# Summing the wide items of the later chunks on GpSimd, in halving additions behind a tile's gathers

## The chip, the cores and the metric

The program runs on one core of one Trainium2 chip. The metric is the device time of one execution, in microseconds (us). The engines are TensorE (PE in the rows, PEld its weight loads), VectorE (DVE), ScalarE (ACT), GpSimd (POOL) and SyncE (SP, which here only issues DMAs).

## The reference

2048 samples with 40 embedding fields of width 64 each. Every pair of fields goes through a 64x64 matrix of its own, and the results go with 16 dense numbers into a small tower:

```python
e = jnp.stack([tbl_0[ids[:, 0]], ..., tbl_39[ids[:, 39]]], axis=1)      # 2048 x 40 x 64
p = inputs[:, rowidx]                                                  # 780 pairs (i < j)
q = inputs[:, colidx]
out = jnp.einsum('bie,fie,bif->bi', p, param, q)                       # param 64 x 780 x 64
h = jnp.concatenate([z, dense_ctx], axis=1)
h = jnp.maximum(h @ W_top1 + b_top1, 0.0)
h = jnp.maximum(h @ W_top2 + b_top2, 0.0)
y = h @ W_top3
```

All of it is in float32.

## The kernel before

The batch is cut into 4 chunks (0 to 3) of 512 samples. Two fields make a tile, so a chunk has 20 tiles; tiles are numbered through the chunks (tile 33 is number 13 of chunk 1). All engines have their instructions written out in program order, and walk through one list of 800 items, 200 in a chunk: 136 "units" and 64 "wides" (v = 0 to 63), which `order(c)` spreads among the units, one wide in about every three items.

**An item** is two matrix products of TensorE into two banks of a ring of 7 PSUM banks (lines 793 and 798), and two multiplications of VectorE that read the banks (lines 668 and 671 for a unit, 685 for a wide). So TensorE can be 7 banks, three and a half items, ahead of VectorE. The products of a unit are summed by TensorE with a matrix of ones (line 816). The products of a wide lie with the samples on the partitions: 128 partitions x 16 columns x 64 elements in `wide_prod`, and the 64 elements have to be summed to one, 16 sums per partition, into `z_b`. Line 606 does that on ScalarE, in 16 activations with an accumulator, four items behind the product. Where `reduced_by_vector` says so, VectorE does it in one TENSOR_REDUCE (line 696) one item behind the product. In chunks 1 to 3 that is every eighth wide: v = 7, 15, 23, 31, 39, 47, 55, 63.

**The slots of wide_prod.** There are 4 (`WIDE_SLOTS`), taken in turn. Before VectorE multiplies wide v + 4 it waits in `wait_reduced` until wide v is summed. VectorE works in order, so whatever stands behind that product waits too.

**The gathers.** GpSimd fetches the rows of a tile with 8 indirect DMAs (line 537), 4 for each of the tile's fields, and waits after each 4 until they have landed. Tiles 4 to 19 of a chunk share three slots of `rows`. Before it gathers into a slot again, GpSimd waits until SyncE's transposing DMA (line 466, semaphore `words_turned`) has read the tile that was in it, three tiles earlier. SyncE issues that transpose from `turn_rows`, no earlier than its place among the weight loads, and those follow TensorE's progress; then four DMAs make planes (line 476), and ScalarE turns them into `e_t` (line 563), which the products read. GpSimd does nothing else after the first microseconds.

Of the kernel before, what the change touches and what calls it, by code (L numbers as in the profile page):

```python
# [8 lines left out]
ALU = mybir.AluOpType  # L9
# [3 lines left out]
P = 128  # L13
E = 64
# [6 lines left out]
CHUNKS = BATCH // NB  # L21
# [6 lines left out]
FIXED = 4  # L28
# [5 lines left out]
WIDES = [(m, t) for m in range(FIXED, TILES) for t in range(BT)]  # L34
NW = len(WIDES)
WIDE_PAIRS = 4 * FIXED
# [6 lines left out]
G_SLOTS = 3  # L43
# [3 lines left out]
WIDE_SLOTS = 4  # L47
# [10 lines left out]
HALVES = WIDE_PAIRS * (TILES - FIXED) // P  # L58
# [24 lines left out]
FIRST_TURNED = 9  # L83
TURN_AHEAD = 10
# [15 lines left out]
def order(c):  # L100

    units = [("unit", u) for u in range(NU)]
    wides = [("wide", v) for v in range(NW)]
    head = sum(m < FIXED for m, _ in UNITS)
    if c > 0:

        items = units[:head]
        spread = NU - head - BEHIND_LAST
        for v in range(NW - 1):
            items += [wides[v]] + units[head + spread * v // (NW - 1):head + spread * (v + 1) // (NW - 1)]  # L110
        return items + [wides[-1]] + units[head + spread:]


    hot = [item for item in units if UNITS[item[1]][0] in ONE_HOT]
    items = hot + units[:head]
    for m in range(FIXED, TILES):
        row = [item for item in units if UNITS[item[1]][0] == m and item not in hot]
        for t in range(BT):
            items += [wides[(m - FIXED) * BT + t]] + row[len(row) * t // BT:len(row) * (t + 1) // BT]
    return items  # L120


ORDERS = [order(c) for c in range(CHUNKS)]
# [3 lines left out]
PLACE = {item: n for n, item in enumerate(ITEMS)}  # L127
# [53 lines left out]
def through(n):  # L181

    return 2 * (n + 1)
# [36 lines left out]
def prep_at(tile):  # L220

    c, m = divmod(tile, TILES)
    if c == 0:

        first = FIRST_OF[0, 5 if m == 4 else max(m, 1)]
        return first if m <= ONE_HOT[-1] else first - m
    return c * NI + TILE_AT[m]
# [24 lines left out]
def reduced_by_vector(c, v):  # L252

    m, t = WIDES[v]
    return c == 0 and (t == 3 and m < 12 or t == 1 and m < 8) or c > 0 and v % 8 == 7


def fixed_slot(c):
# [19 lines left out]
def by_dma(tile):  # L278
    return tile >= FIRST_TURNED
# [5 lines left out]
DMA_TILES = [tile for tile in TILE_ORDER if by_dma(tile)]  # L285
DMA_NUMBER = {tile: n for n, tile in enumerate(DMA_TILES)}
GATHERED = [tile for tile in range(ALL_TILES) if tile not in ONE_HOT]
TILES_AT = {}
for _t in TILE_ORDER:
    TILES_AT.setdefault(prep_at(_t), []).append(_t)  # L290
STEPS_AT = {(_c + 1) * NI + STEP_AT[_s]: (_c, _s) for _c in range(CHUNKS - 1) for _s in range(STEPS)}
# [15 lines left out]
def bank_plan():  # L307
# [3 lines left out]
    for n in range(ALL_ITEMS):  # L311
        takers += [("tile", t) for t in TILES_AT.get(n, ()) if not by_dma(t)]
        if n in STEPS_AT:
# [41 lines left out]
def bilinear_tower(nc, tables, idx, hot_ids, dense_t, weights, w1z, b1c, w2p, b2c, w3c, out):  # L355
    with ExitStack() as ctx:
# [6 lines left out]
        def sem(name):  # L363
            return ctx.enter_context(nc.semaphore(name))
# [9 lines left out]
        wide_prod = sb("wide_prod", [P, WIDE_SLOTS, 2, NB])  # L374
        z_b = sb("z_b", [P, HALVES, BT, P])
# [39 lines left out]
        t_free = sem("t_free")  # L415
        summed = sem("summed")
        reduced_s = sem("reduced_s")
        reduced_v = sem("reduced_v")
        turned = sem("turned")
        z_copied = sem("z_copied")  # L420
        step_ps = sem("step_ps")
# [5 lines left out]
        def wait_reduced(engine, wides):  # L427

            by_vector = sum(reduced_by_vector(*divmod(v, NW)) for v in range(wides))
            if by_vector:  # L430
                engine.wait_ge(reduced_v, by_vector)
            if wides > by_vector:
                engine.wait_ge(reduced_s, wides - by_vector)

        def fields(tiles, slots, t):

# [74 lines left out]
        @block.gpsimd  # L511
        def _(pool):
            nc.gpsimd.memset(ident[:, :], 0.0).then_inc(consts, 1)
            pool.wait_ge(consts, 1)
            nc.gpsimd.affine_select(out=ident[:, :], in_=ident[:, :], compare_op=ALU.not_equal, fill=1.0,
                                    base=0, pattern=[[-1, P]], channel_multiplier=1).then_inc(consts, 1)
            nc.gpsimd.iota(first_row[:, :], [[1, 1]], base=0, channel_multiplier=HOT_J).then_inc(rows_known, 1)
            pool.wait_ge(idx_in, 16)
            for tile in GATHERED:
                c, m = divmod(tile, TILES)  # L520
                slot, use = slot_of(tile)
                if c > 0 and m == 0:
                    pool.wait_ge(idx_in, 16 * (c + 1))
                if m < FIXED and use > 1:

                    pool.wait_ge(t_free, through(PLACE[c - 2, "wide", NW - 1]))
                elif use > 1:

                    last = max(t for t in GATHERED if t < tile and slot_of(t)[0] == slot)
                    if by_dma(last):  # L530
                        pool.wait_ge(words_turned, 16 * (DMA_NUMBER[last] + 1))
                    else:
                        pool.wait_ge(transposed, PE_NUMBER[last] + 1)
                for f in range(2):
                    for t in range(BT):
                        col = (m * 2 + f) * BT + t
                        nc.gpsimd.indirect_dma_start(  # L537
                            out=fields([tile], slice(slot, slot + 1), t)[:, 0, f, :], out_offset=None, in_=tables[m * 2 + f],
                            in_offset=bass.IndirectOffsetOnAxis(ap=idx_now[:, c % 2, col:col + 1], axis=0),
                        ).then_inc(gathered[slot], 16)  # L540
                    if c > 0 or m > 0 or f > 0:

                        pool.wait_ge(gathered[slot], 16 * BT * (f + 1 + 2 * (use - 1)))

        @block.scalar
        def _(act):
# [78 lines left out]
            for n in range(ALL_ITEMS + max(GROUP_LAG) + 1):  # L625
                for tile in TILES_AT.get(n, ()):
                    prepare(tile)
                if n == NI:
                    act.wait_ge(mlp_in, (4 + ZT) * 16)
                if n in STEPS_AT:  # L630
                    finish_step(*STEPS_AT[n])
                if n in TURNS_AT and n < ALL_ITEMS:
                    copy_half(TURNS_AT[n])
                for c, t in Z_ORDER:
                    if t < ZS and group_at(c * GROUPS + Z_FIRST[t + 1] - 1) == n:
                        copy_z(c, t)
                done = n - REDUCE_LAG
                if 0 <= done < ALL_ITEMS and ITEMS[done][1] == "wide":
                    c, _, v = ITEMS[done]
                    if not reduced_by_vector(c, v):  # L640
                        reduce(c, v)
            for half in range(HALVES_ALL):
                if turn_at(half) >= ALL_ITEMS:
# [1 line left out]
            c = CHUNKS - 1  # L645
# [85 lines left out]
        def _(pe):  # L731
# [120 lines left out]
            for n, (c, kind, i) in enumerate(ITEMS):  # L852
                for tile in TILES_AT.get(n, ()):
                    if tile in ONE_HOT:
# [122 lines left out]
```

## Time and profile before

| | us |
|---|---|
| median of the timed runs (3 runs) | 1218.11 |
| lowest and highest | 1217.02, 1220.1 |
| span of the profiled execution | 1255.3 |
| PE busy | 1224.6 (98%) |
| DVE busy | 1053.7 (84%) |
| ACT busy | 972.3 (77%) |
| POOL busy | 573.2 (46%) |

The profiled execution's span, from its first to its last instruction, is 37.2 us longer than the median of the timed runs; no time around the span is given. Times in the rows are us from the start of the span. TensorE's busy time counts overlapped and waiting products and its ends are modelled, so 98% does not mean that it never waits.

### The profile page before, as it was taken

Reading aid. Unit: us, or ns where it says so; the run is one execution under the profiler, and the core shown is the slowest. Engines: PE = TensorE matmul, PEld = TensorE weight load, DVE = VectorE, ACT = ScalarE, POOL = GpSimd, SP = SyncE. Lnnn points to the kernel's source line nnn. Section 1 sums busy time; section 2 is a strip of 40 time slices with the busy share of each in tenths; the row PEclk is TensorE's granted clock in tenths of the full one; section 3 lists DMA queues with packets and bytes.
Section 4 is the critical chain, followed back from the end, with each engine's and each line's share of the span. In section 5 each row is a group of like instructions: output and inputs, shape, how many; then the busy total and the mean of one; then the engine's idle time right before and its main releaser. Section 6 shows DMA issues by size and latency. Waiting matters only on the chain.

```text
span 1255.3 us, 22898 instructions
## 1 busy us (share of the span) xinstructions
PE 1224.6 (98%) x5808; PEld 476.8 (38%) x5808; DVE 1053.7 (84%) x1720; ACT 972.3 (77%) x7177; POOL 573.2 (46%) x607
## 2 busy tenths in 40 slices
PE   6989999999999999999999999999999999999999
PEld 3323433333333333333333433334333334333333
DVE  6858899988888797889998888788999878899980
ACT  0019999975868887898968988799968988899951
POOL 5655554455455555555245555555245555400000
PEclk9988899999999999999999999999999999999999
DMA  7033344433544333333454433333353434122100
GB/s 207 18 113 104 79 119 117 110 104 92 140 100 120 102 104 87 88 81 97 106 134 106 113 84 94 87 80 96 95 155 90 114 97 111 49 63 83 44 1 1
DMA packets 132098, 118.87 MB, mean 95 GB/s; under 512 B 91351, under 2 KB 110039, under 8 KB 131965
## 3 DMA queue, kind: packets, MB, share of 16 engines
q1 hardware_dynamic: 111188, 94.94, 27.3%
q0 software_dynamic: 19200, 19.70, 7.6%
q10 hardware_dynamic: 1576, 2.76, 0.8%
q8 instruction: 46, 0.75, 0.3%
q14 instruction: 88, 0.71, 0.2%
HBM read 80.09 MB, written 0.01 MB: 64 GB/s over the span
## 4 chain that ended last, share of the span: by engine, by line
PE 88%; ACT 7%; issue 2%; DVE 2%; DMA 1%; SPq 0%; ACTq 0%; DVEq 0%
PE ring L793 40%; PE z_ps L816 18%; PE ring L798 17%; PE ring L822 8%; ACT wide_prod L606 6%; PE ring L756 2%; PE ring L826 2%; DVE prod L671 1%; DMA z_t<-tbl 1%; DVE wide_prod L685 0%; ACT e_t L567 0%; PE ring L774 0%; PE ring L829 0%; ACT h L620 0%; PE ring L767 0%
## 5 line engine op out<-in xcount | busy, mean ns | idle before, releaser
L606 ACT ACTIVATE wide_prod<-wide_prod 128x64 f32<-128x64 f32 x3520 | 841.8, 242 | 55.1 <-DVE wide_prod L685 34.8
L537 POOL DMA_INDIRECT rows<-tbl,idx_now x600 | 572.4, 954 | 514.9 <-DMA rows<-tbl,idx_now 310.0
L671 DVE TENSOR_TENSOR prod<-ring,e_t 128x512 f32<-128x512 f32 x1008 | 630.6, 683 | 114.3 <-PE ring L793 97.0
L606 ACT ACTIVATION_READ_ACCUMULATOR wide_prod<-wide_prod 128x1 f32 x3520 | 662.6, 188 | 17.8 <-issue 17.1
L793 PE MATMUL ring<-e_t,w 64*128 64x512 f32 x2176 | 584.3, 613 | 13.6 <-issue 4.8
L685 DVE TENSOR_TENSOR wide_prod<-ring,rows 128x512 f32<-128x512 f32 x512 | 327.8, 682 | 32.1 <-PE ring L798 12.8
L793 PEld LDWEIGHTS ring<-e_t,w 64*128 64x128 f32 x2176 | 229.0, 187 | 326.0 <-issue 210.0
L798 PE MATMUL ring<-w,e_t 64*128 64x512 f32 x1024 | 305.8, 616 | 4.2 <-DVE wide_prod L685 1.8
L816 PE MATMUL z_ps<-prod,strip 128*32 128x512 f32 x2096 | 253.9, 598 | 0.0
L798 PEld LDWEIGHTS ring<-w,e_t 64*128 64x128 f32 x1024 | 116.2, 189 | 150.5 <-issue 85.9
L816 PEld LDWEIGHTS z_ps<-prod,strip 128*32 128x32 f32 x2096 | 55.0, 109 | 179.7 <-issue 117.0
L822 PE MATMUL ring<-z_t,w 128*128 128x512 f32 x224 | 99.8, 598 | 0.0
L563 ACT ACTIVATE e_t<-planes 128x1024 uint16<-128x1024 uint16 x71 | 82.3, 1163 | 12.1 <-DMA planes<-words 12.1
L822 PEld LDWEIGHTS ring<-z_t,w 128*128 128x128 f32 x224 | 41.4, 190 | 56.8 <-issue 47.6
L668 DVE TENSOR_TENSOR prod<-ring,e_t 64x512 f32<-64x512 f32 x80 | 54.8, 685 | 5.9 <-PE ring L793 2.9
L567 ACT ACTIVATE e_t<-ring 128x512 f32<-128x512 f32 x9 | 5.3, 596 | 69.3 <-PE ring L756 38.8
L579 ACT ACTIVATE z_t<-z_ps 128x512 f32<-128x512 f32 x20 | 11.8, 592 | 52.2 <-PE z_ps L816 42.6
L756 PE MATMUL ring<-wide_prod,z_t 125*64 125x512 f32 x160 | 37.6, 618 | 10.7 <-DMA z_t<-tbl 10.3
L696 DVE TENSOR_REDUCE z_b<-wide_prod 128x16 f32<-128x1024 f32 x36 | 43.5, 1209 | 0.0
L615 ACT ACTIVATE h<-ring,b 128x512 f32<-128x512 f32 x16 | 11.0, 686 | 38.8 <-PE ring L822 37.1
L713 DVE TENSOR_SCALAR wide_prod<-w,first_row_f 125x512 f32<-125x512 int32 x56 | 24.5, 492 | 11.4 <-DMA z_t<-tbl 7.9
L826 PE MATMUL ring<-h,w 128*128 128x512 f32 x64 | 29.2, 602 | 0.0
(24 smaller groups left out, 76.4 us busy)
## 6 DMA issues: line engine op xcount, KB each, us to landing
w<-weights SPq DMA_DIRECT2D x64, 768.0 KB
planes<-words SPq DMA_DIRECT2D x284, 64.0 KB
rows<-tbl,idx_now POOLq DMA_INDIRECT x600
z_t<-tbl SPq DMA_DIRECT2D x10, 224.0 KB
w<-weights SPq DMA_DIRECT2D x4, 512.0 KB
w<-hot_ids ACTq DMA_DIRECT2D x7, 256.0 KB
w<-w1z SPq DMA_DIRECT2D x7, 256.0 KB
words<-rows SPq DMA_TRANSPOSE x71
```

What stands on the lines that cost most here:

```text
L537: nc.gpsimd.indirect_dma_start(out=fields([tile], slice(slot, slot + 1), t)[:, 0, f, :], out_offset=None, in_=tables[m * 2 + f], in_offset ...
L563: nc.scalar.activation(e_t[:, m, :].bitcast(U16).rearrange("p (b h) -> p b h", h=2), planes[:, plane_slot, :, :].rearrange("p h b -> p b h ...
L606: last = nc.scalar.activation(products, products, ACT.Copy, accum_out=z_b[:, h, t, col:col + 1])
L668: nc.vector.tensor_tensor(dst[half, 0, :], ring[half, bank, :], e_t[half, m - 1 + j, :], ALU.mult).then_inc(t_free, 1)
L671: nc.vector.tensor_tensor(dst[:, j, :], ring[:, bank, :], e_t[:, k, :], ALU.mult).then_inc(t_free, 1)
L685: nc.vector.tensor_tensor(dst[:, j, :, :, :], src[:, bank, :, :, :], fields(fixed, slice(fixed_slot(c), fixed_slot(c) + FIXED), t), ALU.mu ...
L756: last = nc.tensor.matmul(dst[E * h:E * h + E, :], hot_table[2 * i + h][:, E * j:E * j + E], hot[number % len(hot)], start=j == 0, stop=j ...
L793: nc.tensor.matmul(dst, w[field, slot, P * o:P * o + P], e_t[field, m - 1 if diagonal and b == 0 else m, :], start=True, stop=True).then_i ...
L798: nc.tensor.matmul(dst, e_t[field, m, P * t:P * t + P], w[field, slot, P * o:P * o + FIXED * P], start=True, stop=True).then_inc(t_ready, 1)
L816: last = nc.tensor.matmul(z_ps[32 * col:32 * col + 32, :], strip[:, 30 - 2 * r:62 - 2 * r], prod[:, (c * NU + UNIT_PLACE[c][u]) % PROD_SLO ...
L822: return nc.tensor.matmul(dst, w1[:, t * H1 + P * h:t * H1 + P * h + P], z_t[:, Z_NUMBER[c, t] % Z_SLOTS, :], start=start, stop=stop)
L826: return nc.tensor.matmul(dst, w2[:, k, P * h:P * h + P], h1[:, k, :], start=k == 0, stop=k == KH1 - 1)
```

## The change

The wides v % 8 == 7 of chunks 1 to 3, 24 in all, are no longer summed by VectorE but by GpSimd: six TENSOR_TENSOR additions, in place, each of which adds the upper half of the columns to the lower half (32, 16, 8, 4, 2 and 1 elements wide, 16 columns each); the last writes `z_b`. Between them GpSimd waits for its own preceding addition. The six stand in GpSimd's program behind the eighth gather of a tile that `pool_behind` picks, and ahead of the wait for its landing. `wait_reduced` waits for a third semaphore.

```diff
 def reduced_by_vector(c, v):
     m, t = WIDES[v]
-    return c == 0 and (t == 3 and m < 12 or t == 1 and m < 8) or c > 0 and v % 8 == 7
+    return c == 0 and (t == 3 and m < 12 or t == 1 and m < 8)
+
+def reduced_by_pool(c, v):
+    return c > 0 and v % 8 == 7
...
+POOLED = [(c, v) for c in range(CHUNKS) for kind, v in ORDERS[c] if kind == "wide" and reduced_by_pool(c, v)]
+
+def pool_behind(c, v):
+    n = PLACE[c, "wide", v]
+    behind = max(t for t in GATHERED if t - G_SLOTS < FIRST_TURNED or prep_at(t - G_SLOTS) - TURN_AHEAD <= n + 1)
+    return min(behind + (2 if NW // 2 < v < NW - 1 else 0), GATHERED[-1])
...
             by_vector = sum(reduced_by_vector(*divmod(v, NW)) for v in range(wides))
+            by_pool = sum(reduced_by_pool(*divmod(v, NW)) for v in range(wides))
             if by_vector:
                 engine.wait_ge(reduced_v, by_vector)
-            if wides > by_vector:
-                engine.wait_ge(reduced_s, wides - by_vector)
+            if by_pool:
+                engine.wait_ge(reduced_p, by_pool)
+            if wides > by_vector + by_pool:
+                engine.wait_ge(reduced_s, wides - by_vector - by_pool)
...
+            def fold(c, v):
+                m, t = WIDES[v]
+                h, first = divmod((m - FIXED) * WIDE_PAIRS, P)
+                products = wide_prod[:, (c * NW + v) % WIDE_SLOTS, :, :].rearrange("p j (i e) -> p (j i) e", e=E)
+                if c > 0:
+                    pool.wait_ge(turned, (c - 1) * HALVES + h + 1)
+                pool.wait_ge(t_free, through(PLACE[c, "wide", v]))
+                width = E // 2
+                while width > 1:
+                    nc.gpsimd.tensor_tensor(products[:, :, 0:width], products[:, :, 0:width],
+                                            products[:, :, width:2 * width], ALU.add).then_inc(folded, 1)
+                    folds[0] += 1
+                    pool.wait_ge(folded, folds[0])
+                    width //= 2
+                nc.gpsimd.tensor_tensor(z_b[:, h, t, first:first + WIDE_PAIRS], products[:, :, 0], products[:, :, 1],
+                                        ALU.add).then_inc(reduced_p, 1)
...
                         ).then_inc(gathered[slot], 16)
+                    if f == 1:
+                        for own in ADDED_AT.get(tile, ()):
+                            fold(*own)
                     if c > 0 or m > 0 or f > 0:
                         pool.wait_ge(gathered[slot], 16 * BT * (f + 1 + 2 * (use - 1)))
```

By `pool_behind` the additions for v = 7, 15, 23, 31, 39, 47, 55, 63 stand behind these tiles: in chunk 1 behind 33, 35, 38, 39, 42, 44, 46, 48; in chunk 2 behind 53, 55, 58, 59, 62, 64, 66, 68; in chunk 3 behind 73, 75, 78, and the last five all behind tile 79, the last one gathered.

On GpSimd, from the start of the program; all gathers merge into one row before:

```order
L513 MEMSET ident 128x128
L515 ISA
L515 AFFINE_SELECT ident<-ident 128x128
L517 IOTA first_row 128x1
L537 DMA rows<-tbl,idx_now 128x64 x600
L356 UNCONDITIONAL_BRANCH
```

The same place now, as far as the second group:

```order
L581 DMA rows<-tbl,idx_now 128x64 x232
L555 TENSOR_TENSOR wide_prod<-wide_prod 128x16x32
L555 TENSOR_TENSOR wide_prod<-wide_prod 128x16x16
L555 TENSOR_TENSOR wide_prod<-wide_prod 128x16x8
L555 TENSOR_TENSOR wide_prod<-wide_prod 128x16x4
L555 TENSOR_TENSOR wide_prod<-wide_prod 128x16x2
L560 TENSOR_TENSOR z_b<-wide_prod 128x16
L581 DMA rows<-tbl,idx_now 128x64 x16
```

Behind gather 232, the eighth of tile 33, six additions stand where the next gather stood; 16 gathers (tiles 34 and 35) then come before the next group.

On VectorE, around the sum of wide 7 of chunk 1, with the semaphores that each waits for, before (the first L685 row is the product of wide 7, the second that of wide 8):

```order
L685 TENSOR_TENSOR wide_prod<-ring,rows 128x512 [waits t_ready,reduced_s,reduced_v]
L685 TENSOR_TENSOR wide_prod<-ring,rows 128x512 [waits t_ready]
L671 TENSOR_TENSOR prod<-ring,e_t 128x512 [waits t_ready,summed]
L671 TENSOR_TENSOR prod<-ring,e_t 128x512 [waits t_ready]
L696 TENSOR_REDUCE z_b<-wide_prod 128x16 [waits t_free]
L671 TENSOR_TENSOR prod<-ring,e_t 128x512 [waits t_ready,summed]
L671 TENSOR_TENSOR prod<-ring,e_t 128x512 [waits t_ready]
L685 TENSOR_TENSOR wide_prod<-ring,rows 128x512 [waits t_ready,reduced_s,reduced_v]
```

On VectorE now, a little later: the product of wide 10, a unit, and the product of wide 11, which takes the slot of wide 7.

```order
L732 TENSOR_TENSOR wide_prod<-ring,rows 128x512 [waits t_ready,reduced_s,reduced_v]
L732 TENSOR_TENSOR wide_prod<-ring,rows 128x512 [waits t_ready]
L718 TENSOR_TENSOR prod<-ring,e_t 128x512 [waits t_ready,summed]
L718 TENSOR_TENSOR prod<-ring,e_t 128x512 [waits t_ready]
L732 TENSOR_TENSOR wide_prod<-ring,rows 128x512 [waits reduced_s,t_ready,reduced_p,reduced_v]
L732 TENSOR_TENSOR wide_prod<-ring,rows 128x512 [waits t_ready]
```

The TENSOR_REDUCE is gone, and the product of wide 11 is the first that waits for `reduced_p`, the last of GpSimd's six additions.

## Rows read from the trace of the kernel before

**Rows 1.** The page: engine busy times, and two groups (busy, mean ns; idle before, releaser).
```profile
PE 1224.6 (98%) x5808; PEld 476.8 (38%) x5808; DVE 1053.7 (84%) x1720; ACT 972.3 (77%) x7177; POOL 573.2 (46%) x607
...
L537 POOL DMA_INDIRECT rows<-tbl,idx_now x600 | 572.4, 954 | 514.9 <-DMA rows<-tbl,idx_now 310.0
...
L696 DVE TENSOR_REDUCE z_b<-wide_prod 128x16 f32<-128x1024 f32 x36 | 43.5, 1209 | 0.0
```

**Rows 2.** Timeline of VectorE in chunk 1 (start us, us, what): reduction of wide 7, later wides.
```profile
390.00 1.21 DVE L696 TENSOR_REDUCE z_b<-wide_prod 128x16 f32<-128x1024 f32 x1
...
392.32 1.28 DVE L685 TENSOR_TENSOR wide_prod<-ring,rows 128x512 f32<-128x512 f32 x2
...
399.24 1.28 DVE L685 TENSOR_TENSOR wide_prod<-ring,rows 128x512 f32<-128x512 f32 x2
...
403.07 1.28 DVE L685 TENSOR_TENSOR wide_prod<-ring,rows 128x512 f32<-128x512 f32 x2
...
406.88 1.28 DVE L685 TENSOR_TENSOR wide_prod<-ring,rows 128x512 f32<-128x512 f32 x2
```

**Rows 3.** Timeline of GpSimd: eighth gather of tile 33, first of tile 34.
```profile
423.31 0.95 POOL L537 DMA_INDIRECT rows<-tbl,idx_now  x1 [0.30 <-issue]
426.24 0.94 POOL L537 DMA_INDIRECT rows<-tbl,idx_now  x1 [1.98 <-DMA rows<-tbl,idx_now]
```

**Rows 4.** Timeline of GpSimd: eighth gathers of tiles 35 and 38.
```profile
449.44 0.95 POOL L537 DMA_INDIRECT rows<-tbl,idx_now  x1 [0.31 <-issue]
...
491.42 0.95 POOL L537 DMA_INDIRECT rows<-tbl,idx_now  x1 [0.30 <-issue]
```

**Rows 5.** Timeline of VectorE: products of wides 19 and 27 of chunk 1.
```profile
443.91 0.69 DVE L685 TENSOR_TENSOR wide_prod<-ring,rows 128x512 f32<-128x512 f32 x1
...
474.77 1.28 DVE L685 TENSOR_TENSOR wide_prod<-ring,rows 128x512 f32<-128x512 f32 x2
```

**Rows 6.** Timeline of GpSimd: first gathers of tiles 47, 49; eighth of 53, 58.
```profile
621.99 0.94 POOL L537 DMA_INDIRECT rows<-tbl,idx_now  x1 [22.03 <-DMA words<-rows]
...
652.65 0.94 POOL L537 DMA_INDIRECT rows<-tbl,idx_now  x1 [1.67 <-DMA rows<-tbl,idx_now]
...
716.36 0.94 POOL L537 DMA_INDIRECT rows<-tbl,idx_now  x1 [0.30 <-issue]
...
784.02 0.94 POOL L537 DMA_INDIRECT rows<-tbl,idx_now  x1 [0.30 <-issue]
```

**Rows 7.** Timeline of SyncE: the transpose of tile 44.
```profile
618.19 1.23 SPq L466 DMA_TRANSPOSE words<-rows  x1
```

**Rows 8.** Timeline of VectorE: products of wides 11 and 27 of chunk 2.
```profile
700.25 1.28 DVE L685 TENSOR_TENSOR wide_prod<-ring,rows 128x512 f32<-128x512 f32 x2
...
768.13 1.28 DVE L685 TENSOR_TENSOR wide_prod<-ring,rows 128x512 f32<-128x512 f32 x2
```

**Rows 9.** Timeline of GpSimd in chunk 3: eighth gathers of tiles 73 and 78.
```profile
1007.11 0.94 POOL L537 DMA_INDIRECT rows<-tbl,idx_now  x1 [0.30 <-issue]
...
1074.63 0.94 POOL L537 DMA_INDIRECT rows<-tbl,idx_now  x1 [0.30 <-issue]
```

**Rows 10.** Timeline of VectorE: products of wides 11 and 27 of chunk 3.
```profile
990.67 1.28 DVE L685 TENSOR_TENSOR wide_prod<-ring,rows 128x512 f32<-128x512 f32 x2
...
1058.37 1.28 DVE L685 TENSOR_TENSOR wide_prod<-ring,rows 128x512 f32<-128x512 f32 x2
```

**Rows 11.** GpSimd's other instructions, by group (busy, mean ns; idle before, releaser).
```profile
L515 POOL TENSOR_SCALAR_AFFINE_SELECT ident<-ident 128x128 f32<-128x128 f32 x1 | 0.3, 283 | 0.2 <-POOL ident L513 0.2
...
L517 POOL IOTA first_row<- 128x1 int32 x1 | 0.1, 119 | 0.0
```

**Rows 12.** Busy time by stretch: PE, PEld, DVE, ACT, POOL (count), clock, DMA, GB/s.
```profile
475.00:610.00 135.00, 134.42 (x636) 51.61 (x636) 114.39 (x185) 117.10 (x890) 69.81 (x75) 1.00 0.35 91
```

More of the change, by code:

```diff
@@ L287 @@
 GATHERED = [tile for tile in range(ALL_TILES) if tile not in ONE_HOT]
+POOLED = [(c, v) for c in range(CHUNKS) for kind, v in ORDERS[c] if kind == "wide" and reduced_by_pool(c, v)]
[3 more added lines that the diff above has]
+    return min(behind + (2 if NW // 2 < v < NW - 1 else 0), GATHERED[-1])
+ADDED_AT = {}
+for _c, _v in POOLED:
+    ADDED_AT.setdefault(pool_behind(_c, _v), []).append((_c, _v))
 TILES_AT = {}
@@ L418, in bilinear_tower @@
         reduced_v = sem("reduced_v")
+        reduced_p = sem("reduced_p")
+        folded = sem("folded")
         turned = sem("turned")
@@ L518, in _ @@
             pool.wait_ge(idx_in, 16)
+            folds = [0]
+            def fold(c, v):
[14 more added lines that the diff above has]
+                                        ALU.add).then_inc(reduced_p, 1)
             for tile in GATHERED:
@@ L639, in _ @@
                     c, _, v = ITEMS[done]
-                    if not reduced_by_vector(c, v):
+                    if not reduced_by_vector(c, v) and not reduced_by_pool(c, v):
                         reduce(c, v)
```

## The prediction, made before the changed kernel was run

> **What bounds the kernel now.** I read three views in this order. First the page's busy times [rows 1]: TensorE 98%, VectorE 84%, ScalarE 77%, GpSimd 46%. By these figures the change looks harmless: it takes 24 reductions of 1.209 us, 29.0 us, from VectorE and gives GpSimd, with half of its time free, some work. But the row of the gathers says what the free half is: 514.9 us of idle time, 310.0 of it waiting for gathers to land. GpSimd runs one dependent chain (four gathers, wait, four gathers, wait, next tile) and is late or early as a chain, however idle it looks.
>
> So the second view is the timeline of VectorE around one pooled wide [rows 2], and the third that of GpSimd at the tile behind whose gathers the additions now stand [rows 3]. The reader is to lay them side by side. In chunk 1 the reduction of wide 7 starts at 390.00. The L685 rows behind it are the products of wides 8, 9, 10 and 11, the last at 406.88. Wide 11 takes the slot of wide 7, so by then wide 7 has to be summed. The eighth gather of tile 33 ends at 423.31 + 0.95 = 424.26. That is 17.4 us after VectorE wants the slot, and the additions only begin there. VectorE works in order: behind the product of wide 11 stand all later items; TensorE fills its 7 banks and stops, and ScalarE runs out of products. GpSimd itself waits for nothing that this stalls (tiles 31 to 33 need only transposes that SyncE can issue at items well before wide 11), so the stall ends, but only when GpSimd's chain arrives.
>
> **What the six additions cost.** The trace has no TENSOR_TENSOR on GpSimd, so I bound it. They cover 16 x (32+16+8+4+2+1) = 1008 elements per partition. The nearest rows [rows 11] are a one-input pass over 128 elements, 283 ns, and one over a single element, 119 ns: 0.12 us fixed and (283 - 119)/127 = 1.3 ns per element. The same rows show 0.2 us for a handoff by semaphore between two GpSimd instructions; there are five between the additions and one to VectorE. Low end: at the one-input rate, 1.3 + 6 x 0.12 + 6 x 0.2 = 3.2 us. High end: each addition as long as a gather with its gap, 0.95 + 0.30, makes 7.5 us. I take two inputs at twice the one-input rate, 2.6 + 0.7 + 1.2 = 4.5 us, since that is the row nearest in kind. Call it F.
> The Trainium skill (page "GPSIMD Engine Reference", section "Performance versus the Vector engine") gives 4497 ns for an addition of 2048 float32 elements, 2.2 ns per element, and calls GpSimd the wrong engine for ordinary elementwise work. No row here shows it. Its rate would make F 4.1 us as an estimate, and the whole sum below 11 x 0.4 = 4.4 us smaller.
>
> What one group adds to GpSimd's own chain: before, the next tile's first gather came 1.98 us after the eighth [rows 3] (1.67 in [rows 6]; I use 2.0 with the longer ones among the others), spent on the landing, which now goes on beneath the additions. Then the next gather starts F + 0.3 after the eighth, so each group delays the chain by 4.5 + 0.3 - 2.0 = 2.8 us.
>
> **The sum, chunk by chunk,** as VectorE's delay against before.
> Chunk 1, wide 11: 424.26 + 4.5 - 406.88 = 21.9 us [rows 2, 3]. Wide 15 is summed behind tile 35: 450.39 + 2.8 + 4.5 = 457.7, and wide 19 would now start at 443.91 + 21.9 = 465.8 [rows 4, 5]: no new stall. Wide 23 stands behind tile 38: two groups ahead of it, 492.37 + 5.6 + 4.5 = 502.5, against 474.77 for wide 27 [rows 4, 5]. So VectorE is now late by 27.7 us; a second, smaller stall of about 6.
> In the rest of the chunk GpSimd is early, not late: at tile 47 it waits 22.03 us for the transpose of tile 44 [rows 6], issued at 618.19 [rows 7], which hangs on TensorE's progress. That wait survives: up to there GpSimd's chain is delayed by eight groups at most, or by waiting for products that come 27.7 us late, so it is about as late as VectorE, and the 22 us remain between them. From tile 47 on GpSimd again starts at a fixed distance behind TensorE: the delay of chunk 1 passes on whole, and chunk 2 repeats the pattern.
> Chunk 2, wide 11, with the group behind tile 48 ahead of it: 717.30 + 2.8 + 4.5 - 700.25 = 24.4 us; wide 27, with three groups ahead: 784.96 + 8.4 + 4.5 - 768.13 = 29.7 us [rows 6, 8].
> Chunk 3: 1008.05 + 2.8 + 4.5 - 990.67 = 24.7; 1075.57 + 8.4 + 4.5 - 1058.37 = 30.1 us [rows 9, 10]. Behind tile 79 nothing is gathered, so the last five groups only follow VectorE, each done 4.5 us behind its product with some 15 us to the slot's next use.
> Together 27.7 + 29.7 + 30.1 = 87.5 us.
>
> **What the removed reductions give back.** Those ahead of a stall give nothing, since GpSimd's arrival ends the stall. That leaves v = 31, 39, 47, 55 in each chunk and 63 in chunk 3: 13 x 1.2 = 15.6 us at most. In 475 to 610, VectorE is busy 114.4 of 135 us [rows 12]; there it also waits for TensorE at the tower's products, where a shorter VectorE changes nothing. I take two thirds, 10.4 us. Nothing is charged for GpSimd's additions against VectorE's speed; the bounds of F hold what little there may be.
>
> 87.5 - 10.4 = 77.1 us on the profiled 1255.3. The profiled execution is 3% slower than the timed ones; scaled by 1218.11/1255.3 = 0.970 this is 74.8 us, and 1218.1 + 74.8 = **1293 us**. The sum holds F eleven times (three in chunk 1, four in chunks 2 and 3): F = 3.2 gives 14 us less, F = 7.5 gives 33 more. With the share of the reductions between none and all (+10, -5) the case's own range is 1272 to 1325.
>
> **Rivals.**
> (a) The stalls are much shorter in a timed run than in the profiled one. The 37.2 us between the two need not be spread evenly. From the transpose of tile 44 at 618.19 to the eighth gather of tile 53 at 717.30 GpSimd's chain takes 99.1 us [rows 6, 7]; were it 10% faster when not profiled and VectorE not, each first stall would lose 10 us and the second nearly all: about 12 x 3 = 36 us less, 1257. For it: gathers are issued by GpSimd one by one and may suffer from being recorded. Against: more than 300 us of the chain are landings, which recording need not touch.
> (b) The additions are slow: F about 9, twice mine, because of narrow strided pieces (4, 2, 1 elements) or a change between gather and arithmetic code. Then 11 x 4.5 = 50 us more, plus a stall at wide 43 in each chunk, where VectorE's margin is a few us: about 1345. Against: 0.12 us fixed in [rows 11], and the first gather follows the IOTA without a reload that can be seen.
> The Trainium skill (same page, section "Architecture") says that the first call of freshly loaded code costs about 6 us with no visible instruction. No run here shows it; once, it would come through both stalls of chunk 1 as an estimated +6 us.
> (c) The other side: the stall does not come, since GpSimd reaches the groups in time, and the kernel gets faster. It takes a chain that is 22 us earlier at tile 33, 53 and 73; it decides where the eighth gather of tile 53 plus F falls before 700.25. Then VectorE's 29 us count at two thirds, 19.4, and the time is 1218 - 19 = 1199. Against: three chunks show the same lateness, 17.4, 17.1 and 17.4 us, in one trace, and waiting for the slot is in the program.
> (d) No change to be measured, with a stall that eats just the gain: no mechanism gives that but chance.
>
> **How the numbers follow.** Forecast 0.72, (a) 0.12, (b) 0.10, (c) 0.05, (d) 0.01. The predicted time is the forecast's, 1293. The range 1252 to 1325 holds the forecast's and (a)'s and leaves (b), (c) and (d) out. A measurement of this kernel tells about 0.3% (3.7 us) from no change. Faster: 0.05; within 0.3%: 0.01; slower: 0.94.
>
> **What would show it.** Right: VectorE idle for some 22 us at the product of wide 11 of chunks 1, 2 and 3 and some 6 us at wide 27, put down to GpSimd's last addition; six GpSimd additions that take 4.5 us from the first start to the last end and its handoff; 22 us of waiting at tile 47 still there; VectorE's busy time 29 us shorter. TensorE and ScalarE should show holes at the same places. Wrong: if VectorE's longest waits stay those for TensorE, or if the groups stand in the timeline before the product of wide 11 would come; if F is over 6 us, (b) is on; if the delay of chunk 1 shrinks again before tile 47, the passing on of delays was wrong.

## The result, and the profile after

| | us |
|---|---|
| before, median of 4 runs | 1218.16 |
| changed, median of 4 runs (1309.15 to 1319.41) | 1313.48 |
| ratio, 95% interval | 1.0756 (1.0695 to 1.0817) |
| forecast, range | 1293, 1252 to 1325 |

The change makes the kernel 95 us slower. The direction and the place were forecast; the size was 75 us in the forecast, and 20 us are to be explained. The profile of the changed kernel has a span of 1307.3 us. Its page, to be laid beside [rows 1]:

```profile
PE 1199.4 (92%) x5808; PEld 460.6 (35%) x5808; DVE 1025.7 (78%) x1696; ACT 962.2 (74%) x7177; POOL 649.5 (50%) x751
...
PE   6988999999982999999979699999969599999999
...
PEclk9988899999996999999989799999979799999999
...
L732 DVE TENSOR_TENSOR wide_prod<-ring,rows 128x512 f32<-128x512 f32 x512 | 327.4, 682 | 105.9 <-POOL z_b L560 55.5
```

The reader sees holes in TensorE's row of digits, dips of its granted clock at the same places, and a releaser that was not there before: VectorE's products of wides wait for GpSimd's last addition. VectorE's busy time is 28.0 us shorter, as its 24 missing reductions make it. Whom VectorE waited for in all (us, times, longest):

```profile
DVE prod L718 <- PE ring L840: 117.4, 76, 10.6
DVE wide_prod L732 <- POOL z_b L560: 55.5, 3, 24.9
DVE wide_prod L732 <- issue: 27.6, 8, 8.8
```

The first stall, where [rows 2] had the product of wide 11 at 406.88 with no wait and [rows 3] the eighth gather of tile 33. GpSimd's timeline:

```profile
414.21 0.94 POOL L581 DMA_INDIRECT rows<-tbl,idx_now  x1 [0.30 <-issue]
415.18 3.29 POOL L555 TENSOR_TENSOR wide_prod<-wide_prod 128x512 f32<-128x512 f32 x5
418.55 0.21 POOL L560 TENSOR_TENSOR z_b<-wide_prod 128x16 f32<-128x16 f32 x1
419.25 0.96 POOL L581 DMA_INDIRECT rows<-tbl,idx_now  x1 [0.49 <-issue]
```

VectorE's:

```profile
418.85 1.29 DVE L732 TENSOR_TENSOR wide_prod<-ring,rows 128x512 f32<-128x512 f32 x2 [24.95 <-POOL z_b L560]
```

The additions begin 0.03 us behind the eighth gather, end at 418.76, and VectorE goes on at 418.85: it was waiting for nothing else. The releaser column does not always say so: of the 27.6 us put down to "issue", 23.4 us are three waits at wide 27 (8.8, 7.7 and 6.8 us), and each ends 0.09 us behind a group of additions too. GpSimd's additions by shape (busy, mean ns of one; idle before):

```profile
L555 POOL TENSOR_TENSOR wide_prod<-wide_prod 128x512 f32<-128x512 f32 x24 | 30.5, 1273 | 130.1 <-DVE wide_prod L732 129.8
L555 POOL TENSOR_TENSOR wide_prod<-wide_prod 128x256 f32<-128x256 f32 x24 | 17.5, 728 | 1.9
...
L560 POOL TENSOR_TENSOR z_b<-wide_prod 128x16 f32<-128x16 f32 x24 | 5.1, 215 | 1.9
```

A group takes 3.6 us from first start to last end in each of its 24 places, where I had 4.5.

A wait that I had not forecast is TensorE's, at the turning of `z_b` (L821), where TensorE transposes the sums of the wides. It stands at item 405 for the second half of chunk 1, and at item 605 for that of chunk 2 (items are numbered 0 to 799 through the chunks). In chunk 1:

```profile
648.91 4.56 PE L840 MATMUL ring<-e_t,w 64*128 64x512 f32 x20
663.21 1.09 PE L821 MATMUL ring<-ident,z_b 128*128 128x128 f32 x4 [9.73 <-issue]
```

and on GpSimd, behind tile 48, the sum of wide 63:

```profile
659.51 3.30 POOL L555 TENSOR_TENSOR wide_prod<-wide_prod 128x512 f32<-128x512 f32 x5
662.89 0.21 POOL L560 TENSOR_TENSOR z_b<-wide_prod 128x16 f32<-128x16 f32 x1
```

The trace puts the 9.73 us down to "issue". The sum of wide 63 ends at 663.10 and the turning starts at 663.21: the times give the cause where the releaser column does not.

### The profile page after: what moved, and what is told of

It is laid out like the page before. It is cut to its first block, busy times and chain, and to the rows that moved or that the text cites. A ratio compares the mean times of both kernels' runs of the same rounds, so it can differ in the third digit from the quotient of the medians.

```text
span 1307.3 us, 23229 instructions
## 1 busy us (share of the span) xinstructions
PE 1199.4 (92%) x5808; PEld 460.6 (35%) x5808; DVE 1025.7 (78%) x1696; ACT 962.2 (74%) x7177; POOL 649.5 (50%) x751
## 3 DMA queue, kind: packets, MB, share of 16 engines
q1 hardware_dynamic: 111188, 94.94, 26.4%
## 4 chain that ended last, share of the span: by engine, by line
PE 57%; POOL 17%; issue 12%; DMA 8%; ACT 3%; DVE 1%; SPq 1%; POOLq 0%; DVEq 0%
PE ring L840 24%; POOL rows L581 15%; PE z_ps L863 12%; PE ring L845 11%; DMA rows<-tbl,idx_now 6%; PE ring L869 4%; PE ring L803 3%; ACT wide_prod L653 3%; PE ring L873 2%; DMA words<-rows 2%; POOL wide_prod L555 2%; DVE prod L718 1%; PE ring L876 1%; DMA z_t<-tbl 1%; DMA planes<-words 0%
## 5 line engine op out<-in xcount | busy, mean ns | idle before, releaser
L840 PE MATMUL ring<-e_t,w 64*128 64x512 f32 x2176 | 557.2, 614 | 15.0 <-issue 4.7
L845 PE MATMUL ring<-w,e_t 64*128 64x512 f32 x1024 | 297.2, 614 | 59.9 <-DVE wide_prod L732 59.9
L840 PEld LDWEIGHTS ring<-e_t,w 64*128 64x128 f32 x2176 | 215.7, 189 | 316.6 <-issue 192.6
L863 PE MATMUL z_ps<-prod,strip 128*32 128x512 f32 x2096 | 259.3, 610 | 0.0
L845 PEld LDWEIGHTS ring<-w,e_t 64*128 64x128 f32 x1024 | 112.5, 190 | 202.0 <-DVE wide_prod L732 97.9
L555 POOL TENSOR_TENSOR wide_prod<-wide_prod 128x512 f32<-128x512 f32 (+4 forms) x120 | 72.3, 603 | 137.6 <-DVE wide_prod L732 129.8
L803 PE MATMUL ring<-wide_prod,z_t 125*64 125x512 f32 x160 | 37.8, 622 | 10.8 <-DVE wide_prod L760 10.8
L638 ACT ACTIVATE z_t<-ring 128x512 f32<-128x512 f32 x8 | 4.8, 597 | 38.2 <-PE ring L821 38.2
```

What stands on the lines that cost most here:

```text
L555: nc.gpsimd.tensor_tensor(products[:, :, 0:width], products[:, :, 0:width], products[:, :, width:2 * width], ALU.add).then_inc(folded, 1)
L803: last = nc.tensor.matmul(dst[E * h:E * h + E, :], hot_table[2 * i + h][:, E * j:E * j + E], hot[number % len(hot)], start=j == 0, stop=j ...
L840: nc.tensor.matmul(dst, w[field, slot, P * o:P * o + P], e_t[field, m - 1 if diagonal and b == 0 else m, :], start=True, stop=True).then_i ...
L845: nc.tensor.matmul(dst, e_t[field, m, P * t:P * t + P], w[field, slot, P * o:P * o + FIXED * P], start=True, stop=True).then_inc(t_ready, 1)
L863: last = nc.tensor.matmul(z_ps[32 * col:32 * col + 32, :], strip[:, 30 - 2 * r:62 - 2 * r], prod[:, (c * NU + UNIT_PLACE[c][u]) % PROD_SLO ...
```

## The experiments

The experiments ran on three chips, and the kernel before takes 1218 to 1221 us on one kind and 1250 to 1261 us on another. Every ratio below is against the kernel before, timed on the same chip beside the experiment. VectorE's "lateness" at an item is the start of its first product there, less the start of the same product in the profile of the kernel before: in its new profile for the faster kind of chip, in its first profile for the slower kind. Where an edit takes wides from GpSimd, they go back to VectorE's reduction.

**The kernel before, profiled once more** (no edit).

> The kernel before, unedited, profiled once more. Theory A (the first profile of it was a slow execution by itself, and its extra time has nothing to do with any stage of the change): span near the timed median, 1215 to 1220 us, items of chunk 0 some 11 us earlier than in the first profile, as in the changed kernel's profile, and ScalarE's idle time put down to issue (33 + 17 us) gone. Theory B (recording always costs this kernel 3%): span again near 1255 us.

Measured: 1216.63 us, span 1214.8. Theory A: the first profile, 1255.3 us, was no picture of the timed runs, and item 200 comes 12.0 us earlier here. ScalarE's groups in the first profile:

```profile
L606 ACT ACTIVATE wide_prod<-wide_prod 128x64 f32<-128x64 f32 x3520 | 841.8, 242 | 55.1 <-DVE wide_prod L685 34.8 <-issue 15.7 <-ACT h L620 2.7
L606 ACT ACTIVATION_READ_ACCUMULATOR wide_prod<-wide_prod 128x1 f32 x3520 | 662.6, 188 | 17.8 <-issue 17.1
```

and in the second:

```profile
L606 ACT ACTIVATE wide_prod<-wide_prod 128x64 f32<-128x64 f32 x3520 | 840.7, 241 | 33.3 <-DVE wide_prod L685 32.3 <-DVE prod L671 1.0
L606 ACT ACTIVATION_READ_ACCUMULATOR wide_prod<-wide_prod 128x1 f32 x3520 | 662.2, 188 | 0.0
```

The instructions take the same; in the slower execution ScalarE has pauses between them that nothing explains ("issue", 32.9 us in both rows together). The chips of 1250 to 1261 us show them in each of their profiles (31 to 64 us), and no profile of the faster kind does. So the first profile looks like one from a chip of the slower kind; no record says which chip it was. GpSimd's chain does not get longer with it. Laid beside [rows 2, 3] and [rows 4, 5], wide 11, wide 27 and the eighth gathers of tiles 33 and 38 stand here at

```profile
394.58 1.28 DVE L685 TENSOR_TENSOR wide_prod<-ring,rows 128x512 f32<-128x512 f32 x2
...
458.89 1.28 DVE L685 TENSOR_TENSOR wide_prod<-ring,rows 128x512 f32<-128x512 f32 x2
```

```profile
416.08 0.94 POOL L537 DMA_INDIRECT rows<-tbl,idx_now  x1 [0.31 <-issue]
...
487.56 0.94 POOL L537 DMA_INDIRECT rows<-tbl,idx_now  x1 [0.30 <-issue]
...
600.20 0.94 POOL L537 DMA_INDIRECT rows<-tbl,idx_now  x1 [4.77 <-DMA words<-rows]
```

so GpSimd is late by 22.4 and 29.6 us, not by 17.4 and 17.6, and it waits 4.77 us at tile 47, not 22.03 [rows 6]. At wide 11 of chunks 2 and 3 it is late by 21.4 and 20.3 us.

**Wide 7 alone on GpSimd.** The line is that of `reduced_by_pool`.

```diff
-    return c > 0 and v % 8 == 7
+    return c > 0 and v == 7
```

> Of the eight pooled wides of a chunk only v = 7 stays on GpSimd (chunks 1 to 3), the others go back to VectorE. Theory A (VectorE waits for GpSimd's chain at the product of wide 11): three waits of 22 to 25 us there, 55 to 75 us slower than before, and no wait of TensorE at the turning of z_b. Theory B (the loss is the work of 24 groups on GpSimd, spread evenly): an eighth of it, 12 us slower.

Measured: 1299.71 against 1221.19 us, ratio 1.0658 (1.0626 to 1.0689), +78.5 us with 3 groups instead of 24. VectorE's waits, in three places of its timeline:

```profile
418.93 1.29 DVE L732 TENSOR_TENSOR wide_prod<-ring,rows 128x512 f32<-128x512 f32 x2 [24.37 <-POOL z_b L560]
...
723.87 1.29 DVE L732 TENSOR_TENSOR wide_prod<-ring,rows 128x512 f32<-128x512 f32 x2 [23.77 <-POOL z_b L560]
...
1031.60 1.29 DVE L732 TENSOR_TENSOR wide_prod<-ring,rows 128x512 f32<-128x512 f32 x2 [25.09 <-POOL z_b L560]
```

Theory A. The three waits sum to 73.2 us. Something small comes behind each of them, as the stretches of the wait, of the 15 us behind it and of the next 15 show (busy time by engine; the granted clock is the third figure from the end):

```profile
394.00:419.00 25.00, 2.60 (x12) 0.82 (x8) 0.63 (x2) 6.74 (x49) 16.04 (x20) 0.63 0.33 86
419.00:434.00 15.00, 14.32 (x68) 4.80 (x70) 12.43 (x21) 10.42 (x84) 9.08 (x10) 0.82 0.11 21
434.00:449.00 15.00, 15.00 (x64) 5.90 (x62) 11.68 (x19) 10.87 (x79) 7.02 (x9) 1.00 0.42 103
```

The granted clock is 0.63 in the mean of the wait and 0.82 in that of the 15 us behind it, against 1.00 in the kernel before. Cut finer, behind the wait:

```profile
419.00:423.00 4.00, 3.32 (x10) 0.89 (x14) 4.00 (x7) 2.75 (x23) 2.86 (x3) 0.50 0.08 16
423.00:427.00 4.00, 4.00 (x22) 1.27 (x16) 1.73 (x4) 4.00 (x35) 1.89 (x2) 0.83 0.10 18
427.00:431.00 4.00, 4.00 (x28) 1.24 (x24) 4.00 (x8) 1.00 (x9) 2.84 (x3) 1.00 0.14 27
```

The clock fell to the lower of its two levels while TensorE stood idle, and TensorE works its first 5 us behind the wait at that level (7 to 8 us in the other two chunks). Against the kernel before, VectorE is late by 24.4, 49.3 and 78.0 us at wide 11 of the three chunks and by 26.5, 52.5 and 81.0 us some 20 items later: 2.1 to 3.2 us per stall that come in the first items behind the wait, where the clock is low. These 8.4 us take the loss over the 55 to 75 us of theory A.

**Wide 63 alone on GpSimd.**

```diff
+    return c > 0 and v == 63
```

> Only v = 63 stays on GpSimd. Theory A (in chunks 1 and 2 the group stands behind tiles 48 and 68, and TensorE's turning of the second half of z_b at item 405 and 605 waits for it): two waits of TensorE of about 10 us or more before line 821, 15 to 30 us slower than before; this is the term that my sum lacked. Theory B (only the slots of wide_prod count, and wide 67 wants the slot late enough): no change within 4 us.

Measured: 1241.78 us, ratio 1.0171 (1.0133 to 1.021), +20.6 us. Theory A. TensorE, and GpSimd behind tile 48:

```profile
635.11 1.08 PE L821 MATMUL ring<-ident,z_b 128*128 128x128 f32 x4 [8.68 <-issue]
```

```profile
634.79 0.22 POOL L560 TENSOR_TENSOR z_b<-wide_prod 128x16 f32<-128x16 f32 x1
```

VectorE is 3.65 us late before the first group, where the edit has changed nothing (5.2 us in the next experiment): so much can an execution differ from another. From item 404 to 410 it loses 10.4 us, and 11.4 us from 604 to 610.

**Wides 31, 39, 47 and 55 on GpSimd.**

```diff
+    return c > 0 and v in (31, 39, 47, 55)
```

> Only v = 31, 39, 47, 55 stay on GpSimd, 12 groups in chunks 1 to 3. Theory A (nothing waits for these; VectorE is relieved of 12 x 1.2 = 14.5 us): 5 to 12 us faster than before, GpSimd's wait at tiles 47 and 67 shorter. Theory B (the relief lies beside TensorE's own time): within 3 us of before. Theory C (GpSimd's chain is delayed so far that later tiles come late): slower than before.

Measured: 1253.23 us, ratio 1.0269 (1.0242 to 1.0295), +32.0 us. Slower, as theory C had it, but not by its mechanism of late tiles. Two of VectorE's waits, 13.11 and 12.98 us, carry most of it, one in chunk 1 and one in chunk 2, at the product of wide 43:

```profile
548.26 1.29 DVE L732 TENSOR_TENSOR wide_prod<-ring,rows 128x512 f32<-128x512 f32 x2 [13.11 <-POOL z_b L560]
```

```profile
543.61 0.95 POOL L581 DMA_INDIRECT rows<-tbl,idx_now  x1 [0.31 <-issue]
544.58 3.31 POOL L555 TENSOR_TENSOR wide_prod<-wide_prod 128x512 f32<-128x512 f32 x5
```

Wide 39 stands behind tile 42, and that is too late as well. In the full change it is hidden, because VectorE has already been held up by some 31 us when it comes there. I had taken this stretch for safe from the slow profile. Wide 31, behind tile 39, also makes VectorE wait, 1.2 to 2.2 us at wide 35 of each chunk.

**Only the last of the six additions.**

```diff
-                width = E // 2
+                width = 1
```

> The changed kernel with the last of each group's six additions alone, in the same places and with the same waits; the other five, and so most of the sum, are left out. A group then takes about 0.2 us instead of 3.6. Theory A (the loss is where the groups stand, and each group's length enters each of the chain's stalls, some eleven times in all, and the wait at the turning of z_b in chunks 1 and 2): 30 to 45 us faster than the changed kernel, so about 1275, still 55 to 65 us slower than before. Theory B (the length of the additions is the loss): within 10 us of before, about 1225. Theory C (the length lies under the landings): no different from the changed kernel, 1313.

Measured: 1308.91 against 1260.59 us, ratio 1.0402 (1.0359 to 1.0444), +48 us. The other five additions, and so most of each sum, are left out. Theory A in kind, with a smaller gain than its 30 to 45 us: groups of 0.2 us at these places still lose most of it. Against the changed kernel's 1.0598 on a similar chip (below) the 3.4 us per group are worth about 25 us, seven times 3.4 and not the eleven that I had counted; the two ratios are from different chips.

**All 24 groups behind other tiles.**

```diff
-    return min(behind + (2 if NW // 2 < v < NW - 1 else 0), GATHERED[-1])
+    places = {7: 10, 15: 13, 23: 15, 31: 17, 39: 20, 47: 22, 55: 24, 63: 26}
+    return min(c * TILES + places[v], GATHERED[-1])
```

> All 24 groups, but behind tiles 10, 13, 15, 17, 20, 22, 24, 26 from the start of the chunk (in chunk 3 the last four behind tile 79), where GpSimd's eighth gather ended just behind the product in the new profile of the kernel before. Theory A (placement is most of the loss): no wait of VectorE or TensorE for a group over 3 us, and 60 us or more faster than the changed kernel; what stays is GpSimd's chain, 8 x 2.3 = 18 us longer per chunk against 5 to 11 us of waiting at tiles 47 and 67, so 10 to 35 us slower than before. Theory B (24 groups cost what they cost wherever they stand): as the changed kernel, 1300 and more.

Measured: 1291.11 against 1260.59 us, ratio 1.026 (1.0223 to 1.0297), +30.5 us. Once more on another chip:

> All 24 groups in the re-chosen places, once more; the places come from a trace of a chip where before takes 1220 us. On a slower chip the ratio was 1.026 (31 us). Theory A (the rest of the loss is GpSimd's longer chain against 5 to 11 us of slack at tiles 47 and 67, and the slack is smaller on a fast chip): 30 to 45 us slower than before on a chip of 1220 us, 25 to 35 on a slower one. Theory B (the rest was a bad fit of the places to the slow chip): under 20 us on a chip of 1220 us.

Measured: 1279.18 against 1250.72 us, ratio 1.0229 (1.0181 to 1.0276), +28.5 us. In neither does VectorE's list of waits name GpSimd. Two waits of 1.2 us, at wide 43 of chunks 1 and 2, are put down to "issue" in both runs and end 0.09 us behind a group; all other groups end 3 us or more ahead of the product that takes their slot, and the long stalls are gone. So most of the loss was in the places. What stays is argued and not tested: ScalarE waits for planes, in the second of the two

```profile
ACT e_t L611 <- DMA planes<-words: 58.8, 17, 11.8
```

In the first profile of the kernel before, that was 12.1 us in 7 waits. TensorE waits 25.4 us for the `e_t` that come of them. The gathers come later by GpSimd's additions and by the time it waits for a wide's product (107.7 us in ten waits, of which 23 us lie ahead of the last gather). The loss fits theory A for the slower chips; on a chip of 1220 us it was not tried.

**The 24 wides summed by nobody.**

```diff
-POOLED = [(c, v) for c in range(CHUNKS) for kind, v in ORDERS[c] if kind == "wide" and reduced_by_pool(c, v)]
+POOLED = []
...
-            if by_pool:
-                engine.wait_ge(reduced_p, by_pool)
```

> The 24 wides are summed by no engine: VectorE's reductions are gone and nothing stands in their place; those sums are left out. This is the most that taking them from VectorE can give. Theory A (my prediction's share of two thirds): 29 us x 2/3 = 19 us faster than before. Theory B (they lie beside TensorE's own time, as the small regain behind the stalls of the changed kernel suggests): 3 to 9 us faster.

Measured: 1261.75 against 1260.59 us, ratio 1.0013 (0.999 to 1.0036): neither theory, no gain at all. Once more, on another chip:

> The kernel in which no engine sums the 24 wides (those sums are left out), once more, on the chip of this call. On the chip where before took 1261 us it was not faster at all (ratio 1.0013). Theory A (the reductions lie beside TensorE's and ScalarE's time on every chip): within 4 us of before. Theory B (on a chip where before takes about 1220 us ScalarE is no longer in the way, and VectorE counts): 5 to 15 us faster.

Measured: 1252.44 against 1250.72 us, ratio 0.9993 (0.9968 to 1.0019): theory A. The 29 us on VectorE are worth nothing on these chips. On the faster kind of chip this kernel was not run; the changed kernel's chunk 3 gives a hint there: from wide 35 to the end, VectorE's lateness shrinks by 0.8 us (92.9 to 92.1) while four reductions, 4.8 us, are missing.

**All wides from 31 to 63 of chunk 3 on GpSimd.** The text below speaks of five wides, but the edit drops the condition `v % 8 == 7` and moves 33: the five, and 28 that ScalarE sums in the kernel before.

```diff
+    return c == 3 and v >= 31
```

> Only the last five wides of chunk 3 (v = 31 to 63) are summed by GpSimd, behind the last gather of the program, so that no gather is delayed; all others on VectorE. Theory A: no stall, and 1 to 3 us faster than before, the regain that the changed kernel shows in that stretch. Theory B (a group ends later than the slot or the last turning of z_b wants it): up to 4 us slower.

Measured: 1259.98 us, ratio 1.0015 (0.9989 to 1.004): no change. The trace has 33 groups:

```profile
L560 POOL TENSOR_TENSOR z_b<-wide_prod 128x16 f32<-128x16 f32 x33 | 7.1, 215 | 2.6
```

The stretch from 1100 to 1200 us in the kernel before and here, busy time of TensorE, its weight loads, VectorE, ScalarE and GpSimd:

```profile
1100.00:1200.00 100.00, 100.00 (x515) 37.69 (x515) 93.75 (x153) 93.44 (x733) 0.00 (x0) 1.00 0.20 54
```

```profile
1100.00:1200.00 100.00, 100.00 (x516) 37.44 (x514) 91.43 (x150) 6.58 (x8) 86.00 (x162) 1.00 0.18 51
```

ScalarE's work there is all but gone, VectorE has a little less, GpSimd keeps up, and the time is the same: in this stretch neither ScalarE's sums nor VectorE's reductions set the time on this chip. The five wides by themselves were not run; since 33 groups give nothing, a gain from five is unlikely, and 1 to 3 us could not be told from none.

**The changed kernel on a slower chip, and without wide 63.**

> The changed kernel, unedited, on whichever chip this call gets; the chips differ, since the kernel before takes 1218 to 1221 us in two calls and 1261 in a third. On a chip where before takes about 1220: 1313 again, ratio 1.075. On one where it takes about 1260: theory A (GpSimd's chain has the same length on both and VectorE's items come later on the slow one, so the stalls are shorter): ratio 1.055 to 1.065, as my sum from the slow profile has it, and more than one_addition's 1.040. Theory B (the loss scales with the time): ratio 1.075 on either.

Measured: 1327.03 against 1250.04 us, ratio 1.0598 (1.055 to 1.0645), +77.0 us. Theory A: the same program loses 95 us on one chip and 77 on another. VectorE's waits at wide 11 (the two put down to "issue" also end 0.09 us behind a group):

```profile
427.81 1.29 DVE L732 TENSOR_TENSOR wide_prod<-ring,rows 128x512 f32<-128x512 f32 x2 [21.42 <-POOL z_b L560]
...
743.80 1.29 DVE L732 TENSOR_TENSOR wide_prod<-ring,rows 128x512 f32<-128x512 f32 x2 [14.09 <-issue]
...
1060.56 1.29 DVE L732 TENSOR_TENSOR wide_prod<-ring,rows 128x512 f32<-128x512 f32 x2 [14.20 <-issue]
```

```diff
+    return c > 0 and v % 8 == 7 and (v < 63 or c == 3)
```

> The changed kernel, but wide 63 of chunks 1 and 2 is summed by VectorE as before, the other 22 by GpSimd. Theory A (the turning of z_b waits for the group behind tiles 48 and 68): TensorE's waits of about 10 us before line 821 are gone, and it is 15 to 25 us faster than the changed kernel of this call, if the wait is not only taken over by the stall at wide 11 that follows. Theory B (GpSimd's arrival behind tiles 53 and 73 sets the time there anyhow, so that the wait at the turning is inside it): within 6 us of the changed kernel.

Measured: 1316.26 us on the same chip, ratio 1.0534 (1.0491 to 1.0577), 10.8 us less than the changed kernel: between the theories. The two waits at the turning are gone (before, 10.30 us of idle time at the first), and VectorE's waits at wide 11 of the three chunks are 20.62, 21.20 and 20.75 us instead of 21.42, 14.09 and 14.20. The first two:

```profile
421.11 1.29 DVE L732 TENSOR_TENSOR wide_prod<-ring,rows 128x512 f32<-128x512 f32 x2 [20.62 <-issue]
...
735.14 1.29 DVE L732 TENSOR_TENSOR wide_prod<-ring,rows 128x512 f32<-128x512 f32 x2 [21.20 <-issue]
```

The two spans differ by 12.1 us, but 6.7 of these already stand at wide 11 of chunk 1 (421.11 against 427.81), ahead of any sum of wide 63: GpSimd's gathers came earlier in this execution, by chance as far as the edit goes. The turnings cost 22.5 us of lateness in the changed kernel, and by these two profiles only 5.4 us of them are saved. The rest comes back at the next wide 11, since GpSimd's chain comes when it comes. That is nearer to theory B.

## Why the prediction was right, and where its size was off

VectorE's lateness on the faster chip, put beside the terms of the sum:

| us, chunks 1 to 3 together | forecast, times 0.970 | measured |
|---|---|---|
| stalls at wide 11, with the items just behind | 68.9 | 62.4 |
| turnings of `z_b` | none | 23.9 |
| stalls at wide 27 | 16.0 | 4.9 |
| removed reductions and the rest | -10.1 | 1.7 |
| together | 74.8 | 92.9 |

The first two rows belong together, as said below. Errors of both signs stand in the sum, so that 1293 came within 20 us of 1313 is in part luck.

**The stall at wide 11** was right in place, cause and, for the chip it was read from, in size: 21.9 us forecast for chunk 1, 21.4 us of wait there, 25.0 on the faster chip. Wide 7 alone, with three such stalls, makes 78.5 of the 95 us.

**The stalls were read from a slow execution, and scaled by 0.970,** and this is the step that lost most. I took the stalls to shrink with the rest when the execution is 3% faster. They grow. From the product of wide 11 to the end of the eighth gather I had 17.4, 17.1 and 17.4 us, scaled 50.3 together; the new profile has 22.4, 21.4 and 20.3, together 64.1, so 13.8 us were missing. The reason: between the transpose of tile 44 and the eighth gather of tile 53 GpSimd's chain takes 99.1 us in the first profile [rows 6, 7] and 99.7 in the second, while the way of VectorE from that transpose to wide 11 goes from 82.1 us [rows 7, 8] to 78.2. The wait is a difference between two streams, and only one of them had got faster. The reading has a spread of its own: in the profile with the late wides of chunk 3 on GpSimd, which up to here is the kernel before, GpSimd is late by 21.1 us at wide 11 of chunk 1, against the 17.4 of the first profile.

**The low clock behind each stall** was not in the sum. It came with 2.1, 3.2 and 3.0 us, 8.4 in all, in the run with wide 7 alone.

**Luck on the slower chip.** That the sum on the profile, 77.1 us, equals the 77.0 measured on a chip of that pace is in part luck, as the next points show.

**The length of a group** was 3.6 us, not 4.5. The larger part of the difference is the handoffs, 0.08 us between two additions and 0.09 to VectorE, where I took 0.2 six times. Each addition takes some 0.18 us beside its elements, more than my 0.12. The element rate in the rows above is (1273 - 728)/256 = 2.1 ns, against the 2.6 that I took for twice the one-input rate. The Trainium skill's 2.2 ns (4497 ns for 2048 elements, page "GPSIMD Engine Reference", section "Performance versus the Vector engine") agrees with the trace. Rival (b), slow additions, is out; no first call took longer than the others (3.58 us the first, 3.58 to 3.66 all).

**The second stall, at wide 27,** was there (8.8, 7.7 and 6.8 us), but was not to be added. In the kernel before, TensorE works 6.2 us on a tower step at item 288 and VectorE runs dry there. In the changed kernel TensorE, 7 banks ahead, does that step while VectorE is held up at item 286:

```profile
484.50 6.28 PE L869 MATMUL ring<-z_t,w 128*128 128x512 f32 x14
```

```profile
493.61 1.29 DVE L732 TENSOR_TENSOR wide_prod<-ring,rows 128x512 f32<-128x512 f32 x2 [8.79 <-issue]
```

VectorE's lateness, 26.4 us at item 263 and 34.7 at 286, is back to 30.0 at item 300. Of my 16.5 us for the three second stalls 3.6, 1.1 and 0.2 us stay on the faster chip (lateness at item 300, 500, 700 less that at 263, 463, 663), and nothing in chunk 1 on the slower (21.4 at item 263, 20.6 at 300).

**The wait that the sum lacked** is the turning of `z_b`. I looked up who waits for the slot of a pooled wide and not who else waits for its sum. It costs 10.9 us in chunk 1 and 13.0 in chunk 2 (lateness from item 400 to 410 and from 600 to 610), but most of that is given back at the next wide 11, where the waits are 15.5 and 15.0 us instead of the first one's 25.0. All that the full change adds to wide 7 alone, turnings and second stalls together, is 11.5 us of span (1307.3 against 1295.8, both on the faster kind of chip). On the slower chip 5.4 of 22.5 us stayed, in one pair of profiles.

**The reductions give back nothing:** 10.4 us forecast, 0 measured twice on slower chips; on the faster kind only the hint of chunk 3 (0.8 us) bears on it. VectorE is busy 84% of the time, but it works through 7 banks that TensorE fills, and what it saves it spends idle: ahead of its products it stands idle for 146.4 us in the first profile of the kernel before and for 167.1 in the second profile in which nobody sums, most of it put down to TensorE.

**The bounds of the range** do not follow from their terms: 14 and 5 us below 1293 make 1274, 33 and 10 above it 1336, where the text has 1272 and 1325. 1313 lies inside either.

**The rivals.** (a), shorter stalls in a timed run, had the sign wrong. (c) and (d) are out: GpSimd was late in all three chunks, and the loss is far from none. That delays pass on from chunk to chunk held: VectorE's lateness is 30.0 us at item 300 and 30.7 at item 400, and at tile 47 GpSimd still waits for SyncE's transpose, 9.04 us on the faster chip and 15.62 on the slower.

## What to carry to other kernels

An engine that is 46% busy can still be the last to arrive: before work is put behind an instruction of another engine, lay the two timelines side by side and take the difference at that place, not the idle share. Look up every reader of a moved result, not only the one that the diff names. A stall is a difference between two streams; it doesn't scale with the total, and it has to be read from an execution of the pace that is timed. And count in the trace what an edit has moved: a condition left out turned 5 groups into 33.

## What the runs showed of the hardware

The same program takes 1218 to 1221 us on some chips and 1250 to 1261 on others, at an equal granted clock (0.989 in both profiles of the kernel before) and with equal durations of ScalarE's instructions; what differs is pauses between them that no record explains. What makes them was not settled. GpSimd's additions did not slow VectorE: its products take 682 ns in the mean in the new profile of the kernel before, and 682 ns where GpSimd adds nearly all the time, in the profile with 33 groups from 1100 us on:

```profile
L718 DVE TENSOR_TENSOR prod<-ring,e_t 128x512 f32<-128x512 f32 x114 | 71.1, 682 | 8.5 <-PE ring L840 8.4
```

A semaphore from GpSimd's last addition to VectorE's product took 0.09 us. After each wait of 24 us TensorE worked at the lower of its two clock levels for 5 to 8 us.
